# Tiles 2 to 9 of x come transposed from the host and are centred on GpSimd; means, ScalarE's step, the first residuals and loads are reordered

## What is computed

```
h = max(layernorm(x), 0)                      # mean and variance of each row
norm = ln_weight * h * rsqrt(mean(h^2) + 1e-6)
out = norm @ W_root + bias                    # 1024 -> 286
for r in 0, 1:                                # mean over incoming edges of type r
    out += segment_sum((norm[src] @ W_rel[r]) of type r, dst) / max(count, 1)
x = x + h + elu(out) @ wo                     # 286 -> 1024
h2 = max(layernorm(x), 0)
x = x + gat(h2, W, a)                         # 1024 -> 1024, attention over the same edges
```

## Time and profile before

| | |
|---|---|
| median of 3 runs | 511.51 us (510.75 to 511.76) |
| profiled execution | 510.68 us, span 508.9 us |
| TensorE busy | 491.3 us, 97% of the span |
| VectorE, ScalarE, GpSimd busy | 74%, 45%, 15% |
| granted TensorE clock | full, but for the last slice |

### The profile page before, as it was taken

How to read it: one execution, slowest core, us unless ns; L and a number is a source line. 1 busy time by engine, 2 the same in 40 slices (tenths; PEclk the granted TensorE clock), 3 DMA queues, 4 the chain that set the end, 5 groups by cost and what they waited for, 6 DMA issues and landing times.

```text
span 508.9 us, 7733 instructions
## 1 busy us (share of the span) xinstructions
PE 491.3 (97%) x2953; PEld 422.4 (83%) x2953; DVE 374.2 (74%) x635; ACT 227.4 (45%) x382; POOL 74.9 (15%) x74
## 2 busy tenths in 40 slices
PE   3999999999899999999999999999999999999996
PEld 2889989988889998998788888888888878878785
DVE  4865885599989999997855555556598877777634
ACT  5755543416966666668632222334233323323211
POOL 1182313100000000000000000000083333322400
PEclk9999999999999999999999999999999999999999
DMA  9964264504013334248911111100032232222211
GB/s 254 234 196 129 81 190 127 145 15 114 1 42 109 96 98 147 82 124 300 309 45 42 40 42 43 38 1 0 1 81 82 87 95 62 81 82 81 81 44 44
DMA packets 22186, 49.15 MB, mean 97 GB/s; under 512 B 4798, under 2 KB 10709, under 8 KB 22018
## 3 DMA queue, kind: packets, MB, share of 16 engines
q1 hardware_dynamic: 20879, 44.66, 29.6%
q10 hardware_dynamic: 1008, 3.67, 2.1%
q0 software_dynamic: 256, 0.26, 0.2%
HBM read 33.05 MB, written 16.85 MB: 98 GB/s over the span
## 4 chain that ended last, share of the span: by engine, by line
PE 84%; DVE 7%; DMA 4%; ACT 3%; issue 1%; SPq 0%; ACTq 0%; DVEq 0%
PE ps L1337 11%; PE ps L1605 9%; PE ps L1607 9%; PE ps L1606 9%; PE ps L1502 7%; PE ps L1586 7%; PE ps L1587 7%; PE ps L1588 7%; PE ps L1406 4%; PE ps L1425 2%; DMA xt<-xh_scratch 2%; PE ps L1558 2%; PE ps L1560 1%; PE ps L1559 1%; PE ps L1572 1%; DMA x_scratch<-xt 1%
## 5 line engine op out<-in xcount | busy, mean ns | idle before, releaser
L1605 PE MATMUL ps<-h_hi,att_hi 125*125 125x512 f32 (+1 forms) x190 | 73.6, 387 | 0.0
L1606 PE MATMUL ps<-h_lo,att_hi 125*125 125x512 f32 (+1 forms) x190 | 72.6, 382 | 0.0
L1607 PE MATMUL ps<-h_hi,att_lo 125*125 125x512 f32 (+1 forms) x190 | 72.6, 382 | 0.0
L1586 PE MATMUL ps<-wg,gT_hi 128*125 128x512 f32 x160 | 63.8, 399 | 0.1
L1587 PE MATMUL ps<-wg,gT_hi 128*125 128x512 f32 x160 | 63.1, 395 | 0.0
L1588 PE MATMUL ps<-wg,gT_lo 128*125 128x512 f32 x160 | 63.1, 394 | 0.0
L1502 PE MATMUL ps<-msg_hi,adj_hi 125*125 125x288 f32 x180 | 50.3, 304 | 0.8 <-ACT adj_hi L602 0.8
L1502 PE MATMUL ps<-msg_lo,adj_hi 125*125 125x286 f32 x180 | 45.9, 295 | 0.0
L477 POOL TENSOR_TENSOR some<-first_att 125x625 f32<-125x625 f32 x1 | 2.4, 2441 | 273.3 <-DVE first_att L1162 273.3
L697 ACT ACTIVATE em<-ps,rinv 125x512 f32<-125x512 f32 (+1 forms) x21 | 14.0, 668 | 63.2 <-DVE hp L1208 63.2
L1607 PEld LDWEIGHTS ps<-h_hi,att_lo 125*125 125x125 f32 x190 | 35.3, 186 | 8.0
(11 more groups left out here) (215 smaller groups left out, 1102.3 us busy)
## 6 DMA issues: line engine op xcount, KB each, us to landing
xt<-in_x SPq DMA_DIRECT2D x10, 448.0 KB
xh_scratch<-xt SPq DMA_DIRECT2D x10, 448.0 KB
xt<-xh_scratch SPq DMA_DIRECT2D x10, 448.0 KB
x_scratch<-xt SPq DMA_DIRECT2D x10, 448.0 KB
x1t<-x_scratch SPq DMA_DIRECT2D x10, 448.0 KB
xr<-x_scratch SPq DMA_DIRECT2D x10, 448.0 KB
out_x<-xr SPq DMA_DIRECT2D x19, 224.0 KB
wg_raw<-in_L_gnn_W ACTq DMA_DIRECT2D x7, 512.0 KB, 7.8
```

The lines of the kernel that those rows point to most:

```text
L1586: M.matmul(to, hi, wg[k][:, 0, cut], start=n == 0, stop=False)
L1605: M.matmul(to, hi[:, s, :], h_hi[:, s, cut], start=s == 0, stop=False)
L1606: M.matmul(to, hi[:, s, :], h_lo[:, s, cut], start=False, stop=False)
L1607: return M.matmul(to, lo[:, s, :], h_hi[:, s, cut], start=False, stop=s == TILES - 1)
```

## The change

The host hands over a second input, `x_by_column`: x cut in the same tiles and slices of 128 columns, each transposed ([10, 128, 8, 125]). For tiles 0 and 1 nothing changes. For tiles 2 to 9:

- SP loads the transposed tile too (`load_columns`, 512 KB, one DMA); tiles 2 and 3 ahead of the bias and the edges, the others once the low part two tiles before is done.
- TensorE spreads the tile's means over 128 partitions with one transpose of a broadcast column (`means_spread`) instead of transposing ht.
- ScalarE copies them out of PSUM (`means_out`), GpSimd subtracts them from the transposed tile in place (`centred`), ScalarE takes Relu of that (`raised`) as `hT_hi`, and VectorE takes the low part from the same tile in SBUF. The division by the standard deviation moves to the end: `mean_square` on VectorE multiplies its factor by it.
- `norm` stays (for the residual and the mean square), but nobody transposes its result.
- GpSimd's order: residual(0), centred(2), residual(1), centred(3), residuals 2 and 3, constants, residual(4), then centred(s), residual(s + 1) for s = 4, 5, 6, the gather, and the same for s = 7, 8, 9.
- ScalarE's step becomes messages(s - 2), means_out(s), deviation(s + 1), raised(s), norm(s + 1), mean_square(s + 1).
- TensorE issues means_spread(2) after products_of(0, 5), and tile 0's pieces finish before tile 1's.

```diff
+            def load_columns(t, b):
+                if t >= COLUMNS + 2:
+                    sp.wait_ge(S["hT_lo_rdy"], data(t - 2))
+                sp.dma_start(xc[b][:], x_by_column[t]).then_inc(S["xc_in"][b], 16)
...
             load_x(2, 0)
+            load_columns(2, 0)
             load_x(3, 1)
+            load_columns(3, 1)
             sp.dma_start(bias_b[:], conv_bias.partition_broadcast(T)).then_inc(S["bias_in"], 16)
...
             store_xh(0, 0)
+            load_x(4, 0)
             store_xh(1, 1)
-            load_x(4, 0)
             load_x(5, 1)
+            load_columns(4, 0)
             store_xh(2, 0)
             store_xh(3, 1)
...
             for t in range(AHEAD, TILES):
+                if t + 1 < TILES:
+                    load_columns(t + 1, (t + 1) % 2)
                 store_xh(t, t % 2)
...
-            for t in range(AHEAD):
-                residual(t, t % 2, t // 2)
+            def centred(t, b, d):
+                pool.wait_ge(S["means_rdy"], column(t))
+                pool.wait_ge(S["xc_in"][b], columns_in(t))
+                G.tensor_tensor(xc[b][:], xc[b][:], means[b][:].unsqueeze(1).broadcast_to([P, KT, T]), ALU.subtract).then_inc(S["cent_rdy"], 1)
+            residual(0, 0, 0)
+            centred(2, 0, 1)
+            residual(1, 1, 0)
+            centred(3, 1, 1)
+            residual(2, 0, 1)
+            residual(3, 1, 1)
             more_constants()
-            pipeline((residual, 0), steps=(AHEAD, TILES - 2))
+            residual(4, 0, 2)
+            pipeline((centred, 0), (residual, -1), steps=(AHEAD, TILES - 3))
             gather_windows()
-            pipeline((residual, 0), steps=(TILES - 2, TILES))
+            pipeline((centred, 0), (residual, -1), steps=(TILES - 3, TILES))
...
+            def means_out(t, b, d):
+                act.wait_ge(S["spread_ps"], column(t))
+                if t >= COLUMNS + 2:
+                    act.wait_ge(S["cent_rdy"], column(t - 2))
+                A.copy(means[b][:], bank(b, P, T)).then_inc(S["means_rdy"], 1)
+
+            def raised(t, b, d):
+                act.wait_ge(S["cent_rdy"], column(t))
+                act.wait_ge(S["g_ps"], room(t))
+                A.activation(hT_hi[b][:], xc[b][:], ACT.Relu).then_inc(S["hT_hi_rdy"], 1)
...
             deviation(2, 0)
+            means_out(2, 0, 1)
             norm(2, 0)
+            messages(0, 0, 0)
+            raised(2, 0, 1)
             deviation(3, 1)
+            mean_square(2, 0)
             norm(3, 1)
-            messages(0, 0, 0)
-            transposed(2, 0, 1)
-            mean_square(2, 0)
             mean_square(3, 1)
-            normed(4, 0, 2)
-            messages(1, 1, 0)
+            ahead = lambda part: lambda t, b, d: part(t, b)
+            pipeline((messages, 2), (means_out, 0), (ahead(deviation), -1), (raised, 0), (ahead(norm), -1), (ahead(mean_square), -1), steps=(3, AHEAD))
             pads()
-            pipeline((transposed, 1), (messages, 2), (normed, -1), steps=(AHEAD, TILES + 1))
+            pipeline((messages, 2), (means_out, 0), (ahead(deviation), -1), (raised, 0), (ahead(norm), -1), (ahead(mean_square), -1),
+                     steps=(AHEAD, TILES + 1))
...
             def low_parts(t, b):
                 dve.wait_ge(S["hT_hi_rdy"], data(t))
+                if t >= COLUMNS:
+                    V.scalar_tensor_tensor(hT_lo[b][:], xc[b][:], 0.0, hT_hi[b][:].bitcast(F32), ALU.max, ALU.subtract).then_inc(S["hT_lo_rdy"], 1)
+                    return
...
+                link(V.reciprocal(stats1[:, bass.ds(t, 1), 5], stats1[:, bass.ds(t, 1), 5]))
+                V.tensor_tensor(stats1[:, bass.ds(t, 1), 5], stats1[:, bass.ds(t, 1), 5], stats1[:, bass.ds(t, 1), 2], ALU.mult).then_inc(S["rms_rdy"], 1)
...
             deviation(2, 0)
-            moments(3, 1, 1)
+            variance(3, 1)
             dve.wait_ge(S["bias_rdy"], 1)
             messages(0, 0, 0)
             low_parts(2, 0)
+            deviation(3, 1)
             mean_square(2)
+            messages(1, 1, 0)
             moments(4, 0, 2)
-            messages(1, 1, 0)
...
+            def means_spread(t, b, d):
+                pe.wait_ge(S["var_rdy"], data(t))
...
+                M.transpose(bank(b, P, T), mv[b][:, 0:1].broadcast_to([T, P]), ident[0:T, 0:T]).then_inc(S["spread_ps"], 1)
...
-                pipeline((transposed, 1), (products, 2), steps=(first, end))
+                pipeline((means_spread, 1), (products, 2), steps=(first, end))
...
-            for k in range(2, 7):
+            for k in range(2, 5):
                 products_of(0, k)
                 products_of(1, k)
-            products_of(0, 7)
-            transposed(2, 0, 1)
-            products_of(1, 7)
+            products_of(0, 5)
+            means_spread(2, 0, 1)
+            for k in range(6, KT):
+                products_of(0, k)
+            for k in range(5, KT):
+                products_of(1, k)
```

More of the change, by code:

```diff
@@ L49, in rgcn_gat_kernel @@
     AHEAD = 4
+    COLUMNS = 2
     BAND = 112
@@ L100, in came_x, with column, columns_in @@
         return came(t if t < 2 else t - 2, b)
+    def column(t):
+        return t - COLUMNS + 1
+    def columns_in(t):
+        return (t - COLUMNS) // 2 * 16 + 16
     def left(t, b):
@@ L150, in rgcn_gat_kernel @@
         first_rows_of.close()
+        columns_of = ExitStack()
+        sb(columns_of, "below_xc", [P, 8256], BF16)
+        xc = [sb(columns_of, f"xc{b}", [P, KT, T], F32) for b in range(2)]
+        columns_of.close()
         zero_adj_of = ExitStack()
@@ L194, in rgcn_gat_kernel @@
         assert end1 <= h_end and end2 <= h_end
+        (*means,), end1 = lay(end1, *pairs_of("means", [P, T], F32))
+        assert end1 <= h_end
         (msg_hi, msg_lo), at = lay(h_end, ("msg_hi", [T, TILES, RELS, FP], R32), ("msg_lo", [T, TILES, RELS, F], R32))
@@ L238, in rgcn_gat_kernel @@
         tp_bank = lambda h: ps[:, h, 0:4 * T].rearrange("p (k n) -> p k n", n=T)
-        first_tp = lambda t, h: tp_bank(6 + h if t == AHEAD - 1 else h)
+        first_tp = lambda t, h: tp_bank(h)
         heads = lambda b, h, ends: ps[0:T, 2 if h == 2 else 4 + 2 * b + h, 0:ends[1] - ends[0]]
@@ L262, in rgcn_gat_kernel @@
         S = {n: sem(n) for n in names}
-        for n in ("x_in", "x_ahead", "xh_out", "xh_ahead", "xb_in", "x1_in", "xr_in", "x1_out", "out_done"):
+        for n in ("x_in", "xc_in", "x_ahead", "xh_out", "xh_ahead", "xb_in", "x1_in", "xr_in", "x1_out", "out_done"):
             S[n] = [sem(f"{n}{b}") for b in range(2)]
@@ L506, in norm @@
                 act.wait_ge(S["rstd_rdy"], data(t))
-                act.wait_ge(S["hT_ps"], room(t))
+                if t < COLUMNS + 2:
+                    act.wait_ge(S["hT_ps"], data(t - 2) if t >= COLUMNS else room(t))
                 act.wait_ge(S["xh_rdy"], room(t))
@@ L1360, in transposed @@
                 pe.wait_ge(S["h1_rdy"], data(t))
-                if t != AHEAD - 1:
-                    pe.wait_ge(S["hT_lo_rdy"], room1(t))
+                pe.wait_ge(S["hT_lo_rdy"], room1(t))
                 for k in range(KT):
@@ L1365, in transposed @@
                 last.then_inc(S["hT_ps"], 1)
+            def means_spread(t, b, d):
+                pe.wait_ge(S["var_rdy"], data(t))
+                if t < COLUMNS + 2:
+                    pe.wait_ge(S["hT_lo_rdy"], data(COLUMNS - 1))
+                else:
+                    pe.wait_ge(S["means_rdy"], column(t - 2))
+                M.transpose(bank(b, P, T), mv[b][:, 0:1].broadcast_to([T, P]), ident[0:T, 0:T]).then_inc(S["spread_ps"], 1)
             def products(t, b, d):
@@ L1700, in _ @@
                 second_layer()
[L1702 removed]
+INS = ["x", "x_by_column", "src", "dst", "edge_type_2", "L0_gnn_ln_weight", "L0_gnn_W_rel", "L0_gnn_W_root", "L0_gnn_conv_bias",
        "L0_gnn_wo_weight", "L1_gnn_W", "L1_gnn_a"]
@@ L1711 @@
     arrays, args = {}, []
+    n_tiles, n_slices = 10, 8
+    rows, columns = inputs["x"].shape[0] // n_tiles, inputs["x"].shape[1] // n_slices
+    by_column = np.asarray(inputs["x"]).reshape(n_tiles, rows, n_slices, columns).transpose(0, 3, 2, 1)
     for name in INS:
-        a = np.ascontiguousarray(inputs[name])
+        a = np.ascontiguousarray(by_column if name == "x_by_column" else inputs[name])
         arrays[f"in_{name}"] = a
```

13 lines of the change are left out of this document (7 added, 6 removed).

## The result

The change made the kernel slower: 520.71 us (median of 4 runs, 518.16 to 521.67) against 511.3 for the kernel before on the same chip, a ratio of 1.017 (95% interval 1.0149 to 1.019). Forecast were 517.7 and a range of 511.5 to 522.5. The profiled execution of the changed kernel is the longest of its four, 1.0 us above the median.

What follows compares the result with a forecast made beforehand. TensorE, busy 97% of the span, was taken as the bound. Start 2.5 plus waits 8.4, minus 0.7 of waits already there and 4.0 of transposes, gave +6.2 us: 517.7 for the median, range 511.5 to 522.5.

Steps and rivals of the forecast that it cites:

- main case: Whole kernel: start, waits and saved transposes sum to +6.2 us, 517.7; chance 0.40, own range 515.5 to 519.5.
- more waits: Rival, chance 0.27: VectorE's new multiply loses to centred(6), +9.1 us, 520.6; or the clock falls after the gather, 520.1.
- Transposes, -4.0: TensorE, tiles 4 to 9: eight transposes replaced by one mean spread save 0.66 us a tile, 4.0 us.
- The start, +2.5: Tile 2: two added loads delay the bias, GpSimd's add holds low part(2), products(2) begin at 37.5, 2.5 us later.
- Tile 3 behind GpSimd's queue, wait 2.8: Tile 3: centring comes late, residuals 2 and 3 hold VectorE's low part to 49.8; TensorE waits 2.8 us.
- The edge list, 0.8 and 0.4: VectorE: edge list before low part(5) and picks before low part(6) make TensorE wait 0.8 and 0.4 us.
- The gather, path 13.7, wait 4.1: Tile 7: gather ahead of centred(7) makes a 13.7 us path against 9.6 of cover; TensorE waits 4.1 us.
- The clock: TensorE, within "more waits": long waits lower the clock; covered after the first, about 2.4 us after the gather, 520.1.
- Tile 9, 0.3: Before the last tile, window keys and first rows on VectorE (7.2 us) leave a wait of 0.3 us.
- Faster: Rival, chance 0.09: GpSimd never late, bias within 1 us of today, no waits at tiles 3 to 6; -1.2 us, 510.3.
- No holding: Rival, chance 0.13: GpSimd doesn't stop the long low part, products(2) at 36.2, products(3) without wait, gather stays; +2.3 us, 513.8.

Runs made afterwards that it cites:

- x7_consts: x6_all3 with GpSimd's constants written before it waits for the bias; 509.46 us (ratio 0.9954).
- x4_fill: Changed kernel with useless products on TensorE ahead of two waits, 18 at tile 2 and 12 at tile 7; 518.66 us (ratio 1.0157).
- x3_small: Changed kernel with the one-column multiply and deviation on VectorE written with one SBUF tensor and a per-row scalar; 517.66 us (ratio 1.0137).
- x1_gather: Changed kernel with the gather on GpSimd put behind centred(7) and residual(8); 514.82 us (ratio 1.0068).
- x6_all3: Changed kernel with gather behind centred(7) and residual(8), bias loaded before x's tile 2, and multiply and deviation with one SBUF tensor; 508.25 us (ratio 0.9934).

## Why the prediction was right

Time and sign were right; the sum came out 3.0 us low by the medians. The measured 520.71 lies outside the main case's own range (515.5 to 519.5) and next to the rival "more waits" (520.6 and 520.1), which had a chance of 0.27: the right answer was in part the rival's. In the profiled execution the first stage is 10.8 us longer where the sum had 6.2; the missing 4.6 are mainly 1.1 more wait at tile 5, 1.6 more at tile 6, 1.5 of lower clock in products(7) and 0.8 more at tiles 4 and 9, less 0.5 at tile 3. One step had its mechanism wrong (tile 3), and one cost was left out (the lower clock). By its own steps:

- **Transposes, -4.0.** Right. x7_consts ran the stage at full clock: from products(2) to products(8) 62.28 us (32.56 to 94.84) with 3.5 us of waits, so 58.8 of work. The kernel before needed 63.42 (35.03 to 98.45) with 0.5, so 62.9. That is -4.1 over six tiles. The mean spread delays the next products by 0.03 to 0.13 us (0.12 taken).
- **The start, +2.5.** Measured +2.35, by the mechanism named: bias at 28.51 (28.2), low part(2) held to 36.26 and products(2) at 37.38 (37.5). That it fits to 0.15 us is partly luck, since the bias started between 27.21 and 28.51 in four executions with this order of loads. The lock between a VectorE row with two SBUF operands and GpSimd's add is what the Trainium skill says (SBUF — State Buffer, "Who interferes with whom"), now with the 1000-element row: 2.24 us instead of 1.19.
- **Tile 3 behind GpSimd's queue, wait 2.8.** Wrong in its mechanism: low part(3) took 1.19 and no wait came (x4_fill shows that also with a fast products(2)). I had GpSimd go from residual(2) straight to residual(3); but a VectorE row was already waiting, and it and the low part behind it kept GpSimd out. In x3_small, with no one-column row held, the low part itself waited and came in between (1.70 us, the two residuals 5.72). The extra period was +1.57 all the same, since products(2) ran at the lower clock. The prediction had this loss as covered by the wait; without the wait it was the cost itself.
- **The edge list, 0.8 and 0.4.** Measured 1.85 and 2.0. The rival "more waits" happened here: the multiply lost to centred(6) as it says (1.92), and to residuals at tiles 3 and 4 before (2.17, 2.16). It reached TensorE through the rows behind it on VectorE (messages, moments, then list and picks), less through Relu(6), which I had named. x3_small, which removes just this, ran in 517.66 us with waits of 0.78 and 0.44. This accounts for 2.7 us of the profiled execution (products(4) to products(6), x3_small beside it).
- **The gather, path 13.7, wait 4.1.** From products(6) to products(7) it took 13.66. The wait is 2.34 because products(6) ran at the lower clock, 11.1 us instead of 9.5; in x3_small, at full clock, it is 3.90. The path was right to a tenth although centring was 2.15 and not 2.35.
- **The clock.** Given only inside a rival, as "waits nearly that long", and only after the two long waits. It fell in the 3.80 us wait and cost products(2) 2.4 us, then products(6) and (7) 1.5 each. For the 3.80 us the Trainium skill has it so (TensorE: Matmul & The Clock Gate, "Why this matters for your kernels"). It also fell behind shorter waits, which that section's rule would let pass: 2.34 us at tile 7, and 1.85 at tile 5 in x1_gather; here the measurement decides. The rows do not give a clean limit: x6_all3 lost clock behind 2.63 us, x7_consts did not behind 2.67. x4_fill puts its price in the changed kernel at 1.5 us by the trace and at about 2 by the medians. It belonged into the main case.
- **Tile 9, 0.3:** 0.70.
- **The rivals' sums** do not all come out of their terms. "Faster" is 2.0 and 4.0 against 4.1, which is -1.9 and not -1.2. "No holding" has 2.1 for +2.3, and by its own Relu(3) at 45.4 products(3) would still wait about 0.9. The +9.1 of "more waits" is 6.2 + 2.4 and 0.5 that nothing explains. That its 520.6 meets the measured 520.71 is therefore luck: the multiply was held, but the loss took another path to TensorE, and the clock fell as well.

That 517.66 us of x3_small equals the forecast of 517.7 is partly luck: it contains 3 us of lower clock (products(2) and (7) took 11.1 each) that the sum left out, against a wait at tile 3 that it had in excess.

## What to carry to other kernels

An engine that is nearly idle by its share (GpSimd, 15%) can set the time once a tile's path goes through its queue in order: read what stands ahead of the moved step there, above all waits such as the bias's or the gather's, and count the DMAs that new loads push back. A small operation that competes for a lock costs the length of the other engine's row, so write one-column operations in a form with one tensor and a scalar. Reordering around held rows is a gamble unless one follows everything behind the moved rows; here three single repairs of named waits gained about 3 to 6 us each and added up, and two reorderings lost about 3 and 6.

## What was unexpected of the hardware

- Rows with one tensor of more than one column are held too: the cast of 110x1125 took 0.74 us in the changed kernel and 3.22 in x6_all3, beside GpSimd's add; a 125x2 clamp took 0.17 and 2.33. With one column and a scalar from SBUF they kept 0.21.

```profile
49.23 3.22 DVE L885 CAST edges_f<-edges_i 110x1125 f32<-110x1125 int32 x1
...
83.42 2.33 DVE L921 TENSOR_SCALAR begin<-begin 125x2 f32<-125x2 f32 x1
```

- The lock works both ways: residual(5) took 3.45 us instead of 2.38 (58.11 in GpSimd's rows above); low part(4), 1.20 us, began on VectorE at the same moment and wasn't held.
- Executions of one kernel spread over 3 to 4 us, and not only where TensorE waits: x7_consts took 506.6 to 510.37 in 10 runs, the kernel before, beside it, 509.74 to 513.72 in 25 (1.0 us in the four of the first comparison). A profiled execution can be either end of such a spread.
